# Local attention: preparation moved by two units, and shifted value rows written by two transfers in place of two GpSimd copies

## The reference, cut to what matters

```
h = shift_token(x)                     # the second half of the features comes from the token before
q, k, v = split(h @ wqkv)              # 8 heads of 64
q = rotary_xpos(l2norm(q) * q_scale);  k = rotary_xpos(l2norm(k) * k_scale)
bk, bv = look_around(k), look_around(v)    # windows of 64 tokens, each with the window before it
sim = where(mask, -max, 8 * bq @ bk.T)     # mask: later tokens, and more than 64 back
out = softmax(sim) @ bv
x = x + out @ wo
```

## Time and profile before

| | us |
|---|---|
| median of 3 runs (lowest, highest) | 8063.11 (8062.08, 8072.71) |
| the profiled execution, its own time | 8073.38 |
| its span, first to last instruction | 8071.7 |
| TensorE busy in the span | 5969.8 (74%) |
| VectorE busy | 4107.3 (51%) |
| ScalarE busy | 2971.3 (37%) |
| GpSimd busy | 1953.7 (24%) |

### The profile page before, as it was taken

The page is one execution under the profiler, slowest core; times in us unless marked ns, Lnnn a source line. Parts: engine busy times, 40 slices in busy tenths (PEclk is TensorE's granted clock), DMA queues, the critical chain, the costliest instruction groups (busy, mean ns, idle before and its releaser), DMA issues. The chain is left out here.

```text
span 8071.7 us, 121471 instructions
## 1 busy us (share of the span) xinstructions
PE 5969.8 (74%) x45848; PEld 2884.3 (36%) x45848; DVE 4107.3 (51%) x6441; ACT 2971.3 (37%) x6472; POOL 1953.7 (24%) x1781
## 2 busy tenths in 40 slices
PE   5557567786768876666678999877777798678677
PEld 3445151114442222222234544434344333344343
DVE  4333435662427745888844444344444566444444
ACT  1002323553334541444311222345355355354453
POOL 0113032212142201444511000034143011341341
PEclk6558676887888888787785887889899888899888
DMA  1001012211121100000003221111111000110110
GB/s 44 4 30 51 14 62 68 65 49 64 48 62 43 37 16 14 0 0 0 0 7 64 52 52 44 26 41 38 31 40 38 9 1 1 47 40 15 51 39 23
DMA packets 261161, 268.98 MB, mean 33 GB/s; under 512 B 113600, under 2 KB 190656, under 8 KB 258688
## 3 DMA queue, kind: packets, MB, share of 16 engines
q1 hardware_dynamic: 250368, 240.26, 11.5%
q0 software_dynamic: 10240, 21.25, 0.8%
HBM read 122.59 MB, written 71.66 MB: 24 GB/s over the span
## 5 line engine op out<-in xcount | busy, mean ns | idle before, releaser
L2170 PE MATMUL ps<-s_l2b_hc,ident 128*128 128x512 f32 x512 | 361.4, 846 | 332.6 <-DVE s_l2b_hc L2333 332.6
L1942 DVE TENSOR_REDUCE s_l3l_negmax<-ps 128x4 f32<-128x512 f32 x256 | 175.0, 683 | 744.0 <-PE ps L1783 744.0
L2118 POOL TENSOR_TENSOR s_l2b_Bx<-s_l2b_du,s_l2b_B 128x512 f32<-128x512 f32 x256 | 406.5, 1610 | 473.3 <-ACT s_l2b_B L2240 410.4
L1873 ACT ACTIVATE s_l3l_probs<-ps,s_l3l_biases,s_l3l_q_inverse 128x128 f32<-128x128 f32 x1024 | 455.6, 462 | 55.7 <-DVE s_l3l_biases L1944 55.3
L2325 DVE TENSOR_TENSOR_SCAN s_l2b_state<-s_l2b_decay,s_l2b_Bx 128x512 f32<-128x512 f32 x256 | 389.9, 1562 | 154.6 <-ACT s_l2b_decay L2246 113.3
L1721 POOL TENSOR_TENSOR s_l3l_probs<-s_l3l_probs,s_l3l_inverse 128x512 f32<-128x512 f32 x256 | 266.9, 1043 | 830.5 <-DVE s_l3l_inverse L1923 830.3
L1745 PE MATMUL ps<-s_l3l_hs,s_l3l_wqk 128*128 128x512 f32 x512 | 305.0, 703 | 177.3 <-DVE s_l3l_prod L1897 95.5
L1057 DVE TENSOR_REDUCE s_L3a_negmax<-ps 128x1 f32<-128x128 f32 (+3 forms) x512 | 236.1, 488 | 362.0 <-PE ps L893 359.5
L638 DVE TENSOR_REDUCE s_L1a_negmax<-ps 128x1 f32<-128x512 f32 x512 | 316.5, 681 | 153.3 <-PE ps L501 152.6
L1035 ACT ACTIVATE s_L3a_pt<-ps 128x256 f32<-128x256 f32 (+3 forms) x512 | 195.3, 434 | 530.3 <-PE ps L893 528.5
L908 PE MATMUL ps<-ks,s_L3a_qs 40*128 40x256 f32 (+3 forms) x1024 | 360.2, 610 | 30.1 <-DVE s_L3a_kvsq L1072 16.5
(11 more groups left out here) (658 smaller groups left out, 13547.7 us busy)
## 6 DMA issues: line engine op xcount, KB each, us to landing
s_l3l_qk<-s_l3l_rope SPq DMA_DIRECT2D x1024, 64.0 KB
scratch_rope<-s_L3a_rope SPq DMA_DIRECT2D x32, 512.0 KB, 2.8
ks<-scratch_parts SPq DMA_DIRECT2D x384, 32.0 KB
s_L3a_qs<-scratch_rope SPq DMA_DIRECT2D x64, 128.0 KB
ks<-scratch_rope SPq DMA_DIRECT2D x64, 128.0 KB
s_L0e_slots<-scratch_sent SPq DMA_DIRECT2D x16, 396.0 KB, 5.9
s_L1e_slots<-scratch_sent SPq DMA_DIRECT2D x16, 396.0 KB, 6.3
scratch_square<-s_L1a_rows SPq DMA_DIRECT2D x24, 256.0 KB, 3.0
```

The lines of the kernel that those rows point to most:

```text
L1873: act.activation(t["probs"][:, U % (LAG + 1), k, :], ps[:, U % 2, P * k:P * (k + 1)], ACT.Exp, bias=t["biases"][:, U % (LAG + 1), k:k + 1] ...
L2118: pool.tensor_tensor(t["Bx"][:, n % 2, k, :], t["du"][:, b % 2, k, :], t["B"][:, n % 2, :], ALU.mult).then_inc(s["bx_ready"], 1)
L2170: pe.matmul(ps[:, 4 + k, :], g["ident"][:, :], t["hc"][:, n % 2, k, :], start=(n == 0), stop=(n == STATES - 1)).then_inc(s["summed"], 1)
```

## The change

`prep` is read two units earlier: `beside(b, u)` gives the items of unit u + 2, which in units 6 and 7 are the first two projections of the sequence after the next. The first two projections of sequence 1 run ahead of the first unit. The value tiles are dealt out in another order (3 with `norm`, then 0 and 1, then 2 with `qinv`). GpSimd's `rotate` and `shift` move with them. `stacked` is split into `q_stacked` and `k_stacked`, 16 transfers each. The two copies of `shift_values` are removed; SP writes `vs` with two transfers behind the key transfers of the sequence, when the four value tiles have been taken, and `v_shifted` counts 32 a sequence. The zero rows of `vs` get a semaphore of their own, `zeroed`.

```diff
+    EARLY = 2
     def prep(b, u):
-        if b == BATCH:
+        if not 0 <= b < BATCH:
             return []
         if u < 4:
             return [("proj", b, u, ab) for ab in range(2)]
         if u == 4:
-            return [("norm", b), ("v", b, 1)]
+            return [("norm", b), ("v", b, 3)]
         if u == 5:
-            return [("v", b, 0), ("v", b, 3)]
+            return [("v", b, 0), ("v", b, 1)]
         if u == 6:
             return [("pick", b, 0), ("pick", b, 1)]
         return [("qinv", b), ("v", b, 2)]
+    def beside(b, u):
+        u += EARLY
+        return prep(b + 1 + u // UNITS, u % UNITS)
+    FIRST = [item for u in range(UNITS) for item in prep(0, u)] + [item for u in range(EARLY) for item in prep(1, u)]
...
-        STACKED = 16 * 32
+        STACKED = 16 * 16
...
             for b in range(BATCH):
-                sp.wait_ge(s["stacked"], START + b * STACKED)
+                sp.wait_ge(s["q_stacked"], START + b * STACKED)
+                sp.wait_ge(s["k_stacked"], START + b * STACKED)
                 if b > 1:
                     sp.wait_ge(s["scores_ready"], START + (b - 1) * UNITS)
...
+                for kt in range(4):
+                    taken(sp, ("v", b, kt))
+                sp.dma_start(t["vs"][0:64, b % 2, :, :], t["v"][0:64, b % 2, :, :]).then_inc(s["v_shifted"], 16)
+                sp.dma_start(t["vs"][64:P, b % 2, 1:4, :], t["v"][64:P, b % 2, 0:3, :]).then_inc(s["v_shifted"], 16)
...
-                pool.wait_ge(s["stacked"], START + b * STACKED)
+                pool.wait_ge(s["q_stacked" if e < 2 else "k_stacked"], START + b * STACKED)
...
-            shift_values(0)
+            for e in range(EARLY):
+                rotate(1, e)
             for b in range(BATCH):
                 for u in range(UNITS):
...
-                    if u < 4 and b + 1 < BATCH:
-                        rotate(b + 1, u)
-                    if u == 4 and b + 2 < BATCH:
+                    for ahead, e in ((b + 1, u + EARLY), (b + 2, u + EARLY - UNITS)):
+                        if 0 <= e < 4 and ahead < BATCH:
+                            rotate(ahead, e)
+                    if u == 3 and b + 2 < BATCH:
                         shift(b + 2)
-                if b + 1 < BATCH:
-                    shift_values(b + 1)
...
                 if u == 0:
-                    pe.wait_ge(s["stacked"], START + (b + 1) * STACKED)
+                    pe.wait_ge(s["q_stacked"], START + (b + 1) * STACKED)
+                    pe.wait_ge(s["k_stacked"], START + (b + 1) * STACKED)
...
-                    pe.wait_ge(s["v_shifted"], START + b + 1)
+                    pe.wait_ge(s["zeroed"], START + 1)
+                    pe.wait_ge(s["v_shifted"], START + 32 * (b + 1))
...
-                    for item in prep(b + 1, u):
+                    for item in beside(b, u):
                         side(item)
```

More of the change, by code:

```diff
@@ L1596, in local_attention @@
                "probs": ([P, LAG + 1, 4, P], F32), "turned": ([P, 2, T], F32), "o": ([P, PAIRS, T], F32)}
-    names = ("loaded pool pool_ready tables_ready shifted ready6 ready7 taken6 taken7 squared rope_made rows_floored rows_ready stacked v_shifted "
+    names = ("loaded pool pool_ready tables_ready shifted ready6 ready7 taken6 taken7 squared rope_made rows_floored rows_ready q_stacked k_stacked zeroed v_shifted "
              "scores_ready found max_ready exp_ready inverse_ready probs_ready turned_ready turned_taken pv_done o_taken")
+    EARLY = 2
     def prep(b, u):
-        if b == BATCH:
+        if not 0 <= b < BATCH:
             return []
@@ L1612, in prep @@
         return [("qinv", b), ("v", b, 2)]
+    def beside(b, u):
+        u += EARLY
+        return prep(b + 1 + u // UNITS, u % UNITS)
+    FIRST = [item for u in range(UNITS) for item in prep(0, u)] + [item for u in range(EARLY) for item in prep(1, u)]
     def order():
-        for u in range(UNITS):
-            yield from prep(0, u)
+        yield from FIRST
         for b in range(BATCH):
@@ L1621, in order @@
                     yield ("out", b - 1)
-                yield from prep(b + 1, u)
+                yield from beside(b, u)
         yield ("out", BATCH - 1)
@@ L1673, in _ @@
                             at = 64 * r + 32 * ab
-                            sp.dma_start(t["qk"][at:at + 32, b % 2, 4 * (e // 2) + c, :], t["rope"][32 * k:32 * k + 32, e, ab, :]).then_inc(s["stacked"], 16)
+                            sp.dma_start(t["qk"][at:at + 32, b % 2, 4 * (e // 2) + c, :], t["rope"][32 * k:32 * k + 32, e, ab, :]).then_inc(s["q_stacked" if e < 2 else "k_stacked"], 16)
+                for kt in range(4):
+                    taken(sp, ("v", b, kt))
+                sp.dma_start(t["vs"][0:64, b % 2, :, :], t["v"][0:64, b % 2, :, :]).then_inc(s["v_shifted"], 16)
+                sp.dma_start(t["vs"][64:P, b % 2, 1:4, :], t["v"][64:P, b % 2, 0:3, :]).then_inc(s["v_shifted"], 16)
         @block.gpsimd
@@ L1679, in _ @@
             own(pool.memset(t["hs"][64:P, :, 0:1], 0.0))
-            own(pool.memset(t["vs"][64:P, :, 0, :], 0.0))
+            own(pool.memset(t["vs"][64:P, :, 0, :], 0.0), s["zeroed"], 1)
             own(pool.tensor_copy(t["identb"][:, :], g["ident"][:, :]))
@@ L1811, in values @@
                 mm.then_inc(s["pv_done"], 1)
-            for u in range(UNITS):
-                for item in prep(0, u):
-                    side(item)
+            for item in FIRST:
+                side(item)
             for U in range(BATCH * UNITS + BEHIND):
@@ L1855, in take @@
                         act.wait_ge(s["pv_done"], START + (b - 1) * UNITS)
-                        act.wait_ge(s["v_shifted"], START + b - 1)
+                        act.wait_ge(s["v_shifted"], START + 32 * (b - 1))
                     taken_by(act.activation(t["v"][:, b % 2, kt, :], out, ACT.Copy), item)
-            for u in range(UNITS):
-                for item in prep(0, u):
-                    take(item)
+            for item in FIRST:
+                take(item)
             for U in range(BATCH * UNITS + LAG):
@@ L1946, in _ @@
                     invert(U - 1)
-                    for item in prep((U - 1) // UNITS + 1, (U - 1) % UNITS):
+                    for item in beside((U - 1) // UNITS, (U - 1) % UNITS):
                         if item[0] in ("proj", "norm"):
                             take(item)
-                for item in prep(b + 1, u):
+                for item in beside(b, u):
                     if item[0] in ("pick", "qinv"):
```

## The result

| | median of runs (lowest, highest), us | ratio to before, 95% interval |
|---|---|---|
| before | 8067.91 (8062.08, 8082.16), 4 runs | |
| changed | 7792.62 (7786.03, 7807.33), 4 runs | 0.9659 [0.9639, 0.9678] |

The profiled execution of the changed kernel took 7792.51 us, span 7790.8, granted clock 0.827 over the span (0.813 before). The change saves 3.4%, 275 us between the medians; forecast were 7800 and 264. (The kernel before has one run more in this table than in the one above.)

A forecast was written before the change was run, and what follows sets the result against it. TensorE's wait for the stacking into qk was taken as the bound. Savings of 190 us (middle sequences), 46 (sequence 6) and 28 (sequence 0) make 264, from 8063.1 to about 7800; range 7770 to 7880 for 8 in 10.

The forecast's parts named there:

- The bound and the deadline: First scores of each sequence: TensorE waits for late stacking into qk, 252.1 us in 32 waits; earlier preparation removes it.
- The price of a middle sequence: Eight units, each priced by an old unit with the same work: 46.2 us against 55.7, 9.5 saved.
- The margin: From picks to next scores: 19.1 us of work against 16.3 to 17.6 needed, 1.5 to 2.8 to spare.
- late stacking: Rival: slower key transfers still reach the next scores 3.3 us late; 112 us lost, about 7910, chance 0.10.
- The ends of a call: Sequence 6 saves 11.6 us; sequence 0 saves about 9 less 2 for two projections ahead of the first scores.
- Part 2 at nothing: Shifted values by transfer: relieving GpSimd of 3.35 us a sequence gains nothing; uncovered transfers cost 0 to 8.8, taken 0.
- part 1: Preparation two units earlier: work is dealt out anew and the wait before scores goes; 264 us saved together.
- The reciprocal before `out`: Unit 3: VectorE's 3.35 us reciprocal just clears before `out` is taken; worst case, all exposed, 94 us.
- A feeding engine: Rival: VectorE's reciprocal or its double work in the pick unit is exposed; say 70 us, about 7870, chance 0.12.
- The clock's fall: Rival: short idle times in units 6, 7, 0, 1, 2 lower TensorE's clock; slower, about 8410, chance 0.03.

The follow-up runs named there:

- one_early: The changed kernel with the preparation moved one unit earlier instead of two (EARLY = 1): 7932.57 us, ratio 0.9823.
- values_first: The changed kernel with SP's two transfers of the shifted values put between the query and the key transfers: 8065.84 us, ratio 0.9984.
- early_only: The changed kernel with GpSimd's two copies of the shifted values again in place of the transfers: 7860.21 us, ratio 0.9724.
- the swap: The changed kernel with value tile 1 ahead of tile 0 in unit 3: 7770.25 us, ratio 0.9642.

## Why the prediction was right

**The bound and the deadline: right.** The wait of the first scores on the stacking was what the move removed; one_early and values_first move it by distance and by queue order, and the time follows. The key transfers took 10.96 us, about as long as before (11.26).

**The price of a middle sequence: right, unit by unit.** Predicted 5.80, 5.91, 6.46, 8.92, 4.26, 4.58, 4.38, 5.91 = 46.2; measured 5.80, 5.91, 6.45, 8.86, 4.27, 4.41, 4.26, 5.91 = 45.87. Pricing each unit of the new order by an old unit with the same work held within 0.2 us everywhere. The largest difference, 4.58 against 4.41, is one of reading: the prediction took its units from the starts of band matmuls, and the first of a sequence starts with its weight load, the others 0.4 us behind. By weight loads the old unit 7 without its wait is 4.40; the slow units are 5.96 and 6.71 where the prediction has 6.38 and 7.13.

**The margin: smaller than said.** Predicted 1.5 to 2.8 us to spare. The last key transfer is issued at 5364.91; with the 1.43 us from last issue to scores of before it has landed near 5366.3, an estimate, 1.2 us ahead of 5367.51. The same 0.4 us is missing from the need of 16.3 to 17.6: by weight loads it is 16.7 to 18.1, against 18.85 of work. None of the sequences 1 to 6 had to wait, but late stacking was nearer than the prediction made it.

**The ends of a call: net right, parts off.** Sequence 6 takes 44.4 to 45.3 us, and the weight load behind it waits 3.3 to 4.3 (44.1 and some 3). The two projections ahead of the first unit change the stretch before the first scores by -0.2 to 0.8 us and not by 2. In the first call units 0 and 1 of sequence 0 take 5.29 + 7.51, 2.75 more than before, with a granted clock of 0.78 in unit 1, so this sequence saves 7.1 us there, and 8.4 to 9.7 in the other calls, where 9 less 2 was said. Over the four calls the sequences 1 to 5 save 194 us (190 said), sequence 6 saves 42 (46), sequence 0 with its stretch 33 (28), and sequence 7 another 7, for which nothing was said. That the sum came so near is in part luck: one term too large stands against three too small.

**Part 2 at nothing: the step that failed.** The reason given, that GpSimd still sat idle behind the copies, was read off the old order and used for the new one. On the old order it holds (0.9987). On the new one the copies would have cost 52 us in their old place in GpSimd's order: they fall beside VectorE's small multiplication, where in the old order VectorE's idle time had covered them. The bounds of that step, 0 and a loss of up to 8.8 us a sequence, held no gain at all. The total came out right since the units were priced by old units with no copy in them, so the sum of part 1 held the transfers' gain without naming it: part 1 alone gives 2.8%, the transfers 0.65% more. The time to landing that the prediction bounds by 5.6 to 8.8 us has no row in any run; all that shows is that no matmul on `vs` waited.

**The other rivals.** The reciprocal before `out` does not bind: unit 3 is 8.86 with the same 0.78 wait. A feeding engine does bind in early_only, which is this rival by another way, at 7860 where 7870 was given (that the two are close is chance, the 70 us were put on other work); the transfers are what kept it out of the changed kernel. The clock's fall did not come: 1.00 over the whole sequence, with five idle times of 0.8 to 1.1 us in it. The Trainium skill, "TensorE: Matmul & The Clock Gate", section "A second HAM failure mode: psum-queue depth-cycling", tells of a kernel whose frequent short idle times made it swing; in this trace idle times of that size did not. In early_only the second projection waits 2.35 us, and the clock is 0.92 and 0.85 in one sequence and 1.00 in another.

## What to carry to other kernels

When a wait is removed, ask of each instruction that used to run inside it what it will run beside now: an idle time that covers a copy in the old order is no cover in the new one. A transfer queue that works in order has to be priced with its waits: put in front what has the nearest deadline, and behind it whatever waits for something else. Once the large wait is gone, read the list of waits again: here a second buffer and one reordering brought another 1.7%, and with the swap 2%.

## What the runs showed of the hardware

A small VectorE multiplication whose two operands both lie in SBUF was held to the end of a GpSimd instruction that reads SBUF: 0.17 us alone, 1.47 beside a copy (ending 0.03 us behind it), 0.55 beside the end of another (0.02 behind it), 0.72 beside a rotation (0.02 behind it), and 0.17 again in the middle of a fill, which only writes. The Trainium skill, "SBUF — State Buffer", section "Who interferes with whom", says this: a VectorE instruction with two SBUF inputs contends with a GpSimd instruction that reads SBUF, not with one that only writes it, and the order of issue decides which of the two is blocked. The traces agree, down to an instruction of 512 numbers. VectorE's products beside the second copy, with one operand in the accumulator memory, kept their 0.65 us.

The size of a transfer hardly shows in its usual issue time on SP: the 512 KB and 384 KB into `vs` take 0.50 and 0.60 us in each of 32, the 64 KB into `qk` 0.59 in the median. Single issues take longer, whatever the size: 2.23 us for one of 64 KB, 2.46 for one of 384 KB in values_first.
